# Two experts fed before the last tokens are dispatched, the fallback network behind the experts, scaled halves first

## What is computed

```python
x = x + attention(layernorm(x))
h = layernorm(x)                                   # 2048 rows of 128
probs = softmax(h @ Wr); w_topk, e_topk = top_k(probs, 2)
pos = running count of each expert over (token, choice)
keep = pos < 512
buf[e, pos] = h                                    # 8 x 512 slots
g = rms(buf) * norm_w
buf_out = (gelu(g @ Wg) * (g @ Wu)) @ Wd + buf
combined = h + sum of w_topk * buf_out[e, pos] * keep
fout = gelu(rms(h) * f_norm @ fWg) * (... @ fWu) @ fWd + h
x = x + where(any choice overflowed, fout, combined)
```

## Time and profile before

| what | value |
|---|---|
| median of 3 runs (lowest to highest) | 452.41 us (450.25 to 453.72) |
| the profiled execution's own time | 450.39 us |
| its span, first to last instruction | 448.6 us |
| busy: TensorE / VectorE / GpSimd / ScalarE | 375.8 / 307.7 / 268.4 / 227.7 us |
| granted TensorE clock, mean share of full | 0.957 |

### The profile page before, as it was taken

One profiled execution on the slowest core, in us unless ns is written; L12 is line 12 of the kernel. 1 busy time (PEld: TensorE's weight loads), 2 busy tenths in 40 slices (PEclk: granted clock), 3 DMA queues, 4 the chain that ended last, 5 costly groups with the idle time before them and its releaser, 6 DMA issues.

```text
span 448.6 us, 7214 instructions
## 1 busy us (share of the span) xinstructions
PE 375.8 (84%) x2426; PEld 176.6 (39%) x2472; DVE 307.7 (69%) x717; ACT 227.7 (51%) x508; POOL 268.4 (60%) x243
## 2 busy tenths in 40 slices
PE   8984979999999999999899989997885577998810
PEld 2432434444434334444435333432333253654510
DVE  3786787766777876877875998875387483655514
ACT  1650244767666766666677755767761411222200
POOL 7474084578569778558589358779706250465550
PEclk9998898999999999999999999999999796999985
DMA  8595675003704107906005000004601002222118
GB/s 225 110 278 140 110 146 97 16 1 77 175 2 89 23 0 182 297 13 98 13 1 96 14 2 9 14 7 127 217 12 38 18 30 76 69 69 86 42 45 277
DMA packets 30461, 37.48 MB, mean 84 GB/s; under 512 B 4757, under 2 KB 25045, under 8 KB 30101
## 3 DMA queue, kind: packets, MB, share of 16 engines
q1 hardware_dynamic: 24378, 29.91, 28.3%
q0 software_dynamic: 2240, 4.21, 3.1%
q10 hardware_dynamic: 3808, 2.92, 2.3%
HBM read 28.56 MB, written 12.75 MB: 92 GB/s over the span
## 4 chain that ended last, share of the span: by engine, by line
PE 57%; DVE 16%; DMA 7%; issue 6%; ACT 6%; POOL 5%; another core or an unknown queue 1%; SPq 1%; DVEq 0%; POOLq 0%; ACTq 0%
PE ps_av L1160 14%; PE ps_slot L1039 11%; PE ps_st L1131 11%; DVE neg_max L1381 7%; PE ps_slot L1043 5%; ACT probs L929 3%; PE ps_st L1237 2%; POOL probs L742 2%; PE ps_slot L1191 2%; PE ps_st L1139 2%; DMA q_stack<-parts 2%; DMA x_sb<-in_L_attn_x_dram 2%; PE ps_av L1239 2%; POOL slots L748 2%
## 5 line engine op out<-in xcount | busy, mean ns | idle before, releaser
L929 ACT ACTIVATE probs<-ps_st 128x512 f32<-128x512 f32 (+3 forms) x384 | 168.6, 494 | 105.3 <-PE ps_st L1131 98.3
L1381 DVE TENSOR_REDUCE neg_max<-ps_slot 128x1 f32<-128x640 f32 (+7 forms) x184 | 175.9, 990 | 56.0 <-PE ps_slot L1043 54.1
L742 POOL TENSOR_TENSOR probs<-probs,f_all 128x960 f32<-128x960 f32 (+2 forms) x65 | 123.7, 1904 | 10.3 <-ACT probs L929 5.4
L1039 PE MATMUL ps_slot<-k_stack,q_stack 128*128 128x512 bf16 (+3 forms) x366 | 97.1, 332 | 10.6 <-DVE neg_max L1381 5.3
L1131 PE MATMUL ps_st<-q_stack,k_stack 128*128 128x512 bf16 (+3 forms) x368 | 99.3, 327 | 5.3 <-ACT probs L929 4.5
L1160 PE MATMUL ps_av<-probs,v_all 128*9 128x512 f32 (+3 forms) x768 | 79.8, 488 | 2.5 <-POOL probs L742 1.6
L739 POOL TENSOR_SCALAR_AFFINE_SELECT probs<-probs 128x512 f32<-128x512 f32 x58 | 37.2, 641 | 69.2 <-ACT probs L929 69.0
L1043 PE MATMUL ps_slot<-b_all,flip_b 128*128 128x240 bf16 (+2 forms) x288 | 66.9, 257 | 1.0 <-DVE neg_max L1381 0.5
L1131 PEld LDWEIGHTS ps_st<-q_stack,k_stack 128*128 128x128 bf16 x384 | 34.8, 98 | 75.4 <-ACT probs L929 53.9
L1039 PEld LDWEIGHTS ps_slot<-k_stack,q_stack 128*128 128x128 bf16 x384 | 36.0, 99 | 45.1 <-DVE neg_max L1381 12.8
L814 POOL DMA_INDIRECT parts<-probs,e_tok x32 | 31.2, 974 | 36.0 <-DVE probs L1713 28.7
(11 more groups left out here) (197 smaller groups left out, 408.4 us busy)
## 6 DMA issues: line engine op xcount, KB each, us to landing
q_stack<-q_parts SPq DMA_DIRECT2D x21, 192.0 KB
slots<-in_c_rows_dram SPq DMA_DIRECT2D x4, 528.0 KB, 9.2
probs<-slots SPq DMA_DIRECT2D x8, 264.0 KB
parts<-in_c_rows_dram SPq DMA_DIRECT2D x4, 512.0 KB, 9.3
q_stack<-parts SPq DMA_DIRECT2D x4, 512.0 KB, 5.5
k_stack<-k_parts SPq DMA_DIRECT2D x14, 128.0 KB
f_all<-g_vec ACTq DMA_DIRECT2D x1, 1536.0 KB, 11.4
q_parts<-part_all SPq DMA_DIRECT2D x16, 96.0 KB, 3.5
```

Of the source, the lines that this page charges most:

```text
L742: pool.tensor_tensor(pr, pr, f_of[:, n % (H // HG), :, fo:fo + hi - lo], ALU.mult).then_inc(near_done, 1)
L929: act.activation(probs[:, u % PBUF, g, c0:512], ps_st[:, ST_NO[what] % 3, c0:512], ACT.Exp, scale=SCALE).then_inc(exp_done, 1)
L1039: pe.matmul(ps_slot[:, slot, o + lo:o + hi], q_stack[:, buf, t // MT, g, t % MT * P:(t % MT + 1) * P], k_stack[:, buf, lo // CW, g, 0:hi - ...
L1381: dve.tensor_reduce(neg_max[:, t // MT, heads[0]:heads[-1] + 1, t % MT], src, AX.X, ALU.max, negate=True).then_inc(slot_used, 1)
```

## The change

Experts 0 and 1 no longer wait for the last span. After span 1 has landed, SyncE loads their slots as they stand (`early`). TensorE lays them transposed into PSUM by products with the unit matrix (`lay`), and then adds the tokens of span 2 that go to this expert by products of the tokens' rows with a matrix of zeros and ones (`spread`; VectorE makes the matrix, `one_slot`, by comparing the slot numbers 0 to 511 with the place of each token, `place_of`). GpSimd's first dispatch of span 2 waits for the two early loads. The weights of the slots of experts 0 and 1 are loaded apart once everything has landed (`early_cols`, 128 x 4 x 4 floats out of rows of 132). A table of slot numbers is loaded at the start (`slot_col`).

The fallback network moves behind the last expert, on TensorE, ScalarE and VectorE, with F and G mixed; the idle products in front of the experts are gone. The additions of the normed rows to `x1` go between the gates of the first experts. `scale_rows` works by halves: the first half stands ahead of `gate(e+1, 0)`, and `fold_norm` behind the second half.

```diff
-FALLBACK = [("F", 0), ("F", 1), ("F", 2), ("F", 3), ("G", 0), ("G", 1), ("G", 2), ("G", 3)]
+FALLBACK = [("F", 0), ("F", 1), ("G", 0), ("F", 2), ("G", 1), ("F", 3), ("G", 2), ("G", 3)]
...
+            sp.wait_ge(dispatched, 2 * SPANS[1][1] * 16)
+            for e in range(EARLY):
+                sp.dma_start(early[:, e, :, :], rows_of(e)).then_inc(early_in[e], 16)
             sp.wait_ge(dispatched, 2 * TT * 16)
-            load_slots(0, 0)
-            load_slots(1, 1)
+            load_slots(2, 0)
+            for e in range(EARLY):
+                sp.dma_start(early_cols[:, e, :, :], rows_of(e)[:, :, C:ROW]).then_inc(cols_in[e], 16)
+            load_slots(3, 1)
...
                     pool.wait_ge(u_done, SPANS[SPAN_STARTS[t]][1])
+                    if SPAN_STARTS[t] == 2:
+
+                        for e in range(EARLY):
+                            pool.wait_ge(early_in[e], 16)
...
+            def lay(e):
+
+                bank = ps_slot[:, e, 512:1024]
+                if e == 0:
+                    pe.wait_ge(slot_used, len(SLOT_NO) - 2)
+                pe.wait_ge(early_in[e], 16)
+                for j in range(4):
+                    pe.matmul(bank[:, j * P:(j + 1) * P], early[:, e, j, 0:C], ident, start=(j == 0), stop=False)
+
+            def spread(e):
+
+                bank = ps_slot[:, e, 512:1024]
+                pe.wait_ge(u_done, TT)
+                for t in range(CH):
+                    pe.wait_ge(ones_set, CH * e + t + 1)
+                    mm = pe.matmul(bank, u_rows[:, TT - CH + t, 0:C], one_slot[:, t, :], start=False, stop=(t == CH - 1))
...
-            keep_warm(WARM_SLOTS, ps_av[:, :])
-
-            pe.wait_ge(base_done, TT // 2)
-            turn(0, 0, 0)
+            lay(0)
+            lay(1)
+            spread(0)
+            spread(1)
+
+            pe.wait_ge(exp_done, len(ST_NO))
+            pe.wait_ge(y_evac, 2 * NG)
             gate_up(0, 0, 0)
-            turn(1, 1, 0)
             gate_up(0, 0, 1)
...
+            gate_up(1, 1, 0)
+            pe.wait_ge(slot_used, len(SLOT_NO))
+            down(0, 0)
+            gate_up(1, 1, 1)
+            down(1, 1)
+            turn(2, 0, 0)
+            gate_up(2, 0, 0)
+            turn(3, 1, 0)
+            gate_up(2, 0, 1)
...
+            for e in range(EARLY):
+                for t in range(CH):
+                    if e:
+                        dve.wait_ge(ones_used, (CH - 1) * (e - 1) + t + 1) if t < CH - 1 else dve.wait_ge(eT_ps, e)
+                    dve.tensor_scalar(one_slot[:, t, :], slot_col[:, :], place_of[:, t, e:e + 1], None,
+                                      ALU.is_equal).then_inc(ones_set, 1)
...
+            gate(0, 0, 0)
+            gate(0, 0, 1)
+            add_normed(0, CH)
+            gate(1, 1, 0)
+            gate(1, 1, 1)
+            fold_norm(2, 0)
+            fold_norm(3, 1)
+            add_normed(CH, TT)
             weights_of_rows(0, 0, 0)
...
+            for e in range(EARLY, E_NUM - 2):
+
+                i, n = e % 2, e // 2
+                scale_rows(e, i, n, 0)
+                gate(e + 1, 1 - i, 0)
+                scale_rows(e, i, n, 1)
+                fold_norm(e + 2, i)
+                gate(e + 1, 1 - i, 1)
+                weights_of_rows(e + 2, i, n)
...
+            fallback_act(0)
+            fallback_act(1)
+            add_fallback(0)
+            fallback_act(2)
+            add_fallback(1)
+            fallback_act(3)
+            add_fallback(2)
+            add_rows_of_both(0)
+            add_rows_of_both(1)
+            add_fallback(3)
+            add_rows_of_both(2)
+            add_rows_of_both(3)
```

More of the change, by code:

```diff
@@ L1705, in gate, with scale_rows @@
                 dve.tensor_tensor(gated[i][:, c, :], tmp_g[:, c, :], up, ALU.mult).then_inc(e_gated, 1)
-            def scale_rows(e, i, n):
-                if positive(n):
+            def scale_rows(e, i, n, half):
+                if half == 0 and positive(n):
                     dve.wait_ge(scattered[i], 64 * n)
-                for j in range(4):
-                    dve.wait_ge(eo_ps, 2 * e + j // 2 + 1)
+                dve.wait_ge(eo_ps, 2 * e + half + 1)
+                for j in (2 * half, 2 * half + 1):
@@ L1718, in _ @@
+            scale_rows(0, 0, 0, 1)
             weights_of_rows(1, 1, 0)
[L1719 to L1725 removed]
+            scale_rows(1, 1, 0, 0)
+            scale_rows(1, 1, 0, 1)
+            weights_of_rows(2, 0, 0)
             gate(2, 0, 0)
[L1727 removed]
+            weights_of_rows(3, 1, 0)
             gate(2, 0, 1)
[L1729 removed]
@@ L1730, in _ @@
-            for k in range(1, E_NUM // 2 - 1):
-                fold_norm(2 * k + 2, 0)
-                gate(2 * k + 1, 1, 0)
-                scale_rows(2 * k, 0, k)
-                gate(2 * k + 1, 1, 1)
-                weights_of_rows(2 * k + 2, 0, k + 1)
-                fold_norm(2 * k + 3, 1)
-                gate(2 * k + 2, 0, 0)
-                scale_rows(2 * k + 1, 1, k)
-                gate(2 * k + 2, 0, 1)
-                weights_of_rows(2 * k + 3, 1, k + 1)
-            gate(E_NUM - 1, 1, 0)
@@ L1742, in _ @@
-            scale_rows(E_NUM - 2, 0, E_NUM // 2 - 1)
-            gate(E_NUM - 1, 1, 1)
-            scale_rows(E_NUM - 1, 1, E_NUM // 2 - 1)
-            for c in range(NCH):
+            for e in range(EARLY, E_NUM - 2):
[6 more added lines that the diff above has]
+                weights_of_rows(e + 2, i, n)
@@ L1747, in _, with add_rows_of_both @@
+            e = E_NUM - 2
+            scale_rows(e, 0, e // 2, 0)
+            gate(e + 1, 1, 0)
+            scale_rows(e, 0, e // 2, 1)
+            gate(e + 1, 1, 1)
+            scale_rows(e + 1, 1, e // 2, 0)
+            scale_rows(e + 1, 1, e // 2, 1)
+            def add_rows_of_both(c):
                 r = slice(c * CH, (c + 1) * CH)
```

201 lines of the change are left out of this document (106 added, 95 removed).

## The result

The changed kernel takes 446.92 us (median of 4 runs, 445.69 to 448.28) where the kernel before takes 451.33 (4 runs): a ratio of 0.9913, 95% interval 0.9884 to 0.9942. Measured again later, beside the last experiments, it was 446.87 against 450.98, 0.9893 (0.984 to 0.9946). So it is faster by about 4 us; whether by more than 1% these two measurements leave open. The prediction was 446.7.

What follows compares the result with a forecast made beforehand. The first expert was taken to wait for a dispatch, not an engine. `down(7)` at 422.25, plus 17.9 and 2.73, ends at 442.9 against 448.6; 5.7 off the 452.4 median gives 446.7, range 443.0 to 450.3.

Steps and rivals of the forecast that it cites:

- The early loads, `lay` and `spread`: Experts 0 and 1 on TensorE ahead of the first `gate_up`: `lay` from 354.4 to 358.3, `spread` done at 365.6.
- the cover of 2.3 us: GpSimd's new wait for the early loads ahead of span 2's dispatch at 357.08 costs nothing, with 2.3 us to spare.
- early loads late: Rival, chance 0.07: early loads take 5.6 instead of 2.55, `lay` comes 3.0 later, giving 449.7 us.
- `turn(2)` waits for VectorE: Expert 2's first transposes start at 381.8, TensorE waiting from about 377.6 for VectorE's queued work, including 12 additions (3.2).
- The clock: TensorE's idling ahead of `turn(2)` slows its clock afterwards: 2.8 us lost, bounds 0 and 3.25.
- no slow stretch: Rival, chance 0.16: TensorE keeps its clock over the gap ahead of `turn(2)`, 2.8 us less, 443.9 us.
- The period: One steady expert falls from 6.64 to 5.87 us, as halved scaling removes TensorE's 0.77 wait before `turn`.
- four periods 23.5: Term for the steady experts between `down(2)` and `gate_up(7,1)`: four steps of 5.87, 23.5 us in the sum.
- The tail: After `down(7)`: fallback 11.25, then pairs' additions of 1.4 four times with 1.06 among them, 17.9 us in all.
- The fallback's price of 0.95: Moving the fallback behind the last expert lengthens the tail after `down(7)` from 16.97 to 17.9, costing 0.95 us.
- the tail at half clock: Rival, chance 0.10: TensorE runs the fallback after `down(7)` at half clock, 8.84 becoming 17.7, giving 455.5 us.
- The total: Span's end at 442.9 against 448.6, 5.7 less; taken from the median of 452.4, 446.7 us.

Runs made afterwards that it cites:

- the pair of traces: The changed kernel (446.92 us) and the same with 14 idle products on TensorE between `down(1)` and `turn(2)` (449.14 us).
- the kernel without the slow stretch: Changed kernel with 14 idle products of 128x512 on TensorE between `down(1)` and `turn(2)`: 449.14 us, ratio 0.9974 to before.
- the additions later: Changed kernel with VectorE's 12 additions put behind expert 2's scaling, three in each of four steady experts: 444.98 us, ratio 0.9882 to before.
- after again: The changed kernel with nothing altered, measured again beside the last experiments: 446.87 us against 450.98 before, ratio 0.9893.

## Why the prediction was right, and where it was not

**The early loads, `lay` and `spread`: right.** Counted from span 2's dispatch, `lay` stands 2.8 ahead of it and `spread` ends 7.9 behind it; the prediction's 354.4 and 365.6 against 357.08 are 2.7 ahead and 8.5 behind. A comparison takes 0.45 (five in 2.25) where 0.6 was taken from bounds of 0.35 and 0.70; all that TensorE pays is 0.31 ahead of `spread`, for the first of them. GpSimd's wait at its dispatch is released by VectorE (7.73), not by the new wait for the loads: the cover of 2.3 us held. The rival "early loads late" is out.

**`turn(2)` waits for VectorE: right, and now shown.** Predicted 24.7 behind the dispatch (381.8), measured 23.86; the 12 additions take 3.23 (3.2). Taking the additions away moves it by 3.15.

**The clock: right in the forecast, and its price of 2.8 is 2.88 in the pair of traces.** The row that spoke for the rival "no slow stretch", from 430 to 434 in before, is followed by this one:

```profile
434.00:438.00 4.00, 0.00 (x0) 0.00 (x0) 0.00 (x0) 0.00 (x0) 0.38 (x1) 0.52 0.22 49
```

So the clock fell behind that idle stretch too, where no product was left to pay for it. What the prediction did not say, and what this rival took for granted, is that these 2.9 us are not there to be won alone: the kernel without the slow stretch is not 2.8 us faster but 2.2 slower. Expert 2's down products then fall into the row of scatters, which takes the 2.9 back, and the tail costs 1.4 more. That it is the scatters was shown with the additions later, not in this kernel.

**The period: right as a mechanism, mis-sized as a sum.** The steps are 5.85, 6.06 and 7.12 (in after again 5.85, 5.84 and 6.66) where three times 5.87 was predicted. The long one is a scaling that starts 2.43 after its `down` (410.84 to 413.27) instead of 1.2: the late word again, behind a row of four scatters (TensorE's update is recorded at 413.14, for products that end at 412.00). The term "four periods 23.5" came out 1.4 too short, and 0.7 in after again; taking the halves away costs 1.8, not 3.1.

**The tail: 18.46, predicted 17.9.** The product behind the last F ends at 435.87, 10.8 after `down(7)`, where the sum had 10.2: F and G do not run quite back to back. What follows takes 7.6 (7.7). The fallback's price of 0.95 is 1.5 in the profiles of before and after, and 1.8 by experiment. The slower rival, the tail at half clock, did not come: an F takes 1.76 (424.99 to 426.75).

**The total.** From the dispatch to the span's end after is 4.6 us shorter than before (91.5 to 86.9) and 5.4 the second time, predicted 5.7. The medians differ by 4.4 and 4.1. The difference may lie ahead of the dispatch, which begins 2.2 and 1.5 later in these two profiles than in that of before; with one execution each this is not shown. That 446.7 lies so near to 446.9 is in part luck: the median of before that the saving was taken from, 452.4 of three runs, came out as 449.8 to 451.3 in later and longer rows of runs. The saving was 1.3 to 1.6 us too large, and the base 1.1 or more too high, and the two errors nearly cancel.

Where the saving sits, the prediction did not ask. The halves alone, a change of VectorE's order, give 0.9923 where the whole change gives 0.9913 and 0.9893. What the early loads and the moved fallback together add to them, 0.5 to 1.4 us by these ratios, is not clear of the intervals.

## What to carry to other kernels

When a wait for data is removed, list what the engine that comes next in line still has queued, and move whatever nobody needs yet into its idle time: here 16 additions moved into such time, with one scaling and one `turn` moved up, were worth as much as the whole change. A slow stretch of the clock can hide another limit that shows when the clock is kept, so price it by running without it, not by its rows alone. And count savings from a row that both profiles share (here the first dispatch of span 2), since what lies ahead of it moved by up to 3.3 us from profile to profile.

## What the runs showed of the hardware

The engines that wait for TensorE can go on late while GpSimd issues indirect DMAs one behind the other, though TensorE's own rows go on, because TensorE's semaphore updates come late. An update that is not held is recorded 0.01 us behind the end of its product (24 in after); held ones come later, by 1.1 us in after (413.14) and by up to 5.0 with the additions later (392.58). With the additions later VectorE idles 3.7 at the second half of `down(2)`, and ScalarE goes on 4.2 behind the end of `turn(4)`; without the eight scatters before them neither is held. In the routing it is 4.5 in before (350.61) and 2.0 in after (353.11), but that the dispatches cause it there was not tried.

A row of issues isn't enough for it, since after itself runs expert 2 through such a row (383.62 to 393.57) without a hold, with the granted clock at 0.50 from 384 to 388 and at 0.77 in the mean from 388 to 392; and gaps of 0.7 us weaken it at one place and not at the other. What the path is on which the update waits, these traces do not show.
